# Eight feature tiles in the ring, the first query stack filled head by head, denominators turned before they are inverted

## The chip, the cores and the metric

One core of a Trainium2 chip. The metric is the device time of one execution in microseconds; the kernel before has 1396.77 us (median of 3 runs, 1396.46 to 1396.88).

## The reference

A layer on x of shape 8 x 1024 x 512 (8 batches, 1024 tokens, 512 features), all in float32: linear attention with random features, 16 heads of 32 columns and 128 features a head, then a ternary linear layer, with a layer norm after each.

```python
def feature_map(x, orf):                       # orf: 128 x 32
    proj = x @ orf.T / 32 ** 0.25
    norm = jnp.sum(x * x, axis=-1, keepdims=True) / (2.0 * math.sqrt(32))
    return (jnp.exp(proj - norm) + 1e-6) / math.sqrt(128)

q = feature_map(split(x @ Wq.T + bq), orf)     # split: 16 heads
k = feature_map(split(x @ Wk.T + bk), orf)
v = split(x @ Wv.T + bv)
kv, ksum = jnp.einsum('nlm,nld->nmd', k, v), jnp.sum(k, axis=1)
out = einsum('nlm,nmd->nld', q, kv) / einsum('nlm,nm->nl', q, ksum)
x = layernorm(x + out @ Wo.T + bo)
x = layernorm(x + x @ (ternary(W) * scale).T)
```

The division by the query features' product with ksum is the denominator of which the change speaks.

## The kernel before

Precision comes from splitting: a float32 operand is held as a high part rounded to fp32r and the rest as a low part, and three fp32r products (hi x hi, lo x hi, hi x lo) replace one float32 product. The features of a head are made from a stack in SBUF: rows of the projected unit's high and low parts and of its norms lie under one another, so that one or two matrix products give projection and norm together.

One list of stages, `SCHEDULE`, is walked by every engine's program in the same order, and each engine does its own part of a stage; so the list is the order of the instructions on every engine, and semaphores tie them. A batch is eight units: heads in four groups g, for each group a key unit (even u) and a query unit (odd u), and then the output stages. The lines that matter:

- `P` (L858): projection of a later unit, in four pieces of six products spread over a unit; `S` (ACT L582, L585) and `L` (DVE L756) take its high part, squares and low part out of PSUM. PSUM gives two banks to P, V, O and FF in turn.
- `LIFT` (SP, L427 to L451): copies the unit's high and low parts by DMA into the stack of its parity, 10 DMAs for a key unit and 12 for a query unit. `N` (PE L866, DVE L764 and L767) makes the norms and POOL's or SP's queue lifts them (L316, four DMAs). For unit 1 the wait is that of `NL`, and both wait for the last `FF` of the batch before (L434, L514), since the output stages use the same half of `ST` for the split attention (columns 0 to 2047) and the split rows (2048 to 3071); heads 0 to 3 of the stack lie at columns 0, 1024, 2048 and 3072.
- `F`: feature tile r of 0 to 7. PE makes the exponents (key: L821 with orf_key_a and orf_key_b, four products; query: L885, one), ACT takes the exponential (L601) into the ring `FE` of four tiles, and for a key unit DVE adds the tile to a running sum in `DR[:, 0]` (L718, L721). A key's tile r is one of token block r, a query's is head r % 4 of token half r // 4.
- `G` r (PE L898): 16 narrow float32 matmul records for two tiles, 128 x 32 weights, kv += features x values; the last, G 7, also multiplies the sum with ones (L904). In a key unit the pairs G 0,1, G 2,3 and G 4,5 stand between pieces of P and pairs of F; G 6,7 stand in the query unit after its F 0,1.
- `KVT` (PE L912, L913; DVE L771): kv and ksum turned; `GG` half (PE L927, 16 records): numerators into `ND[half]` and denominators into `DN`, four heads' 512 tokens each, every denominator repeated on its head's 32 partitions.
- After `GG`, ACT copies `DN` into `DR[:, h]` and adds the eps term (L621); stage `R` on DVE inverts 128 x 512 (L785) and multiplies (L787) into `VA`. In the last query unit and the output stages R comes in two halves of 256 columns.
- Output stages per token block: `A` split, `O` output product (L821 with Wo), `LN` (DVE L799 to L708, POOL L500, L502), `Y` and `ST` (ACT L549), `YT` transposes (PE L943, ACT L629, DVE L804), `FF` (L821 with W_ternary, DVE L809), and `V` (L844 to L846) of the next batch between them. In batch 0, unit 2 ends with `WF`, the ternary weights, on DVE (L693, L694).

## Time and profile before

| | us |
|---|---|
| median of 3 runs | 1396.77 |
| the profiled execution, its own time | 1395.43 |
| its span on the core (granted clock 0.991) | 1392.9 |
| PE busy, span share | 1335.7, 96% |
| DVE busy | 949.0, 68% |
| ACT busy | 741.5, 53% |
| POOL busy | 318.5, 23% |

The engines are PE (TensorE's products), PEld (its weight loads, beside PE), DVE (VectorE), ACT (ScalarE), POOL (GpSimd) and SP (SyncE, here a DMA queue). Products overlap: a product of 512 columns is shown 0.39 us long while the next starts 0.23 us after it, so that a stall is best read from the distance of two starts. A row of the timeline that merges instructions gives the start of the first and the end of the last. A batch takes 167.2 us in the middle of the run.

### The profile page before, as it was taken

Reading aid. Unit: us, or ns where it says so; the run is one execution under the profiler, and the core shown is the slowest. Engines: PE = TensorE matmul, PEld = TensorE weight load, DVE = VectorE, ACT = ScalarE, POOL = GpSimd, SP = SyncE. Lnnn points to the kernel's source line nnn. Section 1 sums busy time; section 2 is a strip of 40 time slices with the busy share of each in tenths; the row PEclk is TensorE's granted clock in tenths of the full one; section 3 lists DMA queues with packets and bytes.
Section 4 is the critical chain, followed back from the end, with each engine's and each line's share of the span. In section 5 each row is a group of like instructions: output and inputs, shape, how many; then the busy total and the mean of one; then the engine's idle time right before and its main releaser. Section 6 shows DMA issues by size and latency. Waiting matters only on the chain. (4 is left out here: it accounts for less than half of the span.)

```text
span 1392.9 us, 25111 instructions
## 1 busy us (share of the span) xinstructions
PE 1335.7 (96%) x9034; PEld 957.8 (69%) x9034; DVE 949.0 (68%) x1594; ACT 741.5 (53%) x1401; POOL 318.5 (23%) x573
## 2 busy tenths in 40 slices
PE   6999999999999999999999999999999999999885
PEld 5656677666776677666786667866677666776564
DVE  5468774787657776667756777567774687647684
ACT  5457535665355743557436663467535665355542
POOL 1011231113221222212322114211231112321232
PEclk9999999999999999999999999999999999999997
DMA  6566504673147720668116761267503673146511
GB/s 206 135 152 150 135 32 111 155 180 95 38 120 177 177 67 35 150 151 197 46 35 158 186 156 44 77 144 180 147 31 104 158 178 100 39 120 145 129 46 45
DMA packets 85562, 164.55 MB, mean 118 GB/s; under 512 B 20416, under 2 KB 37440, under 8 KB 84928
## 3 DMA queue, kind: packets, MB, share of 16 engines
q1 hardware_dynamic: 68480, 140.04, 39.5%
q10 hardware_dynamic: 9792, 17.12, 3.4%
q0 software_dynamic: 7168, 5.80, 3.2%
q8 instruction: 72, 1.18, 0.4%
q14 instruction: 50, 0.41, 0.1%
HBM read 39.13 MB, written 16.78 MB: 40 GB/s over the span
## 5 line engine op out<-in xcount | busy, mean ns | idle before, releaser
L601 ACT ACTIVATE features<-ps 128x512 f32<-128x512 f32 x512 | 278.1, 597 | 218.5 <-PE ps L821 166.9
L785 DVE RECIPROCAL den<-den 128x512 f32<-128x512 f32 (+1 forms) x80 | 216.6, 2708 | 44.6 <-ACT den L621 44.6
L316 POOL DMA_DIRECT2D stacks<-norm_rows x224 | 121.9, 550 | 542.9 <-DVE norm_rows L767 514.0
L721 DVE TENSOR_TENSOR den<-den,features 128x512 f32<-128x512 f32 x192 | 140.4, 731 | 93.5 <-ACT features L601 82.5
L500 POOL TENSOR_TENSOR stats<-stats,cols 128x1 f32<-128x1 f32 x128 | 79.3, 619 | 451.7 <-DVE stats L708 451.7
L821 PE MATMUL ps<-Wo_hi,stacks 128*128 128x512 f32 x512 | 173.4, 402 | 1.4 <-DVE rows L799 0.7
L574 ACT ACTIVATE values_then_attention<-ps 128x512 f32<-128x512 f32 x64 | 38.3, 599 | 196.6 <-PE ps L846 193.1
L821 PE MATMUL ps<-orf_key_a,stacks 128*128 128x256 f32 x512 | 140.8, 307 | 0.0
L821 PE MATMUL ps<-W_ternary,stacks 128*128 128x512 f32 x512 | 129.5, 396 | 7.2 <-DVE stacks L804 7.2
L927 PE MATMUL ps<-features,kv_ksum 128*32 128x512 f32 x1024 | 126.1, 610 | 5.2 <-DVE kv_ksum L771 3.4
L549 ACT ACTIVATE rows<-rows,stats 128x512 f32<-128x512 f32 x128 | 101.0, 813 | 54.8 <-POOL stats L502 54.6
L821 PE MATMUL ps<-orf_key_b,stacks 72*128 72x256 f32 x512 | 128.1, 281 | 0.0
L756 DVE SCALAR_TENSOR_TENSOR unit_lo<-ps,cols,unit_hi 128x512 fp32r<-128x512 f32 x128 | 95.5, 746 | 44.4 <-ACT squares L585 43.7
L821 PEld LDWEIGHTS ps<-Wo_hi,stacks 128*128 128x128 f32 x512 | 96.4, 188 | 34.4 <-issue 13.8
L821 PEld LDWEIGHTS ps<-orf_key_a,stacks 128*128 128x128 f32 x512 | 96.7, 189 | 29.4 <-issue 29.1
L821 PEld LDWEIGHTS ps<-W_ternary,stacks 128*128 128x128 f32 x512 | 96.8, 190 | 29.0 <-issue 5.1
L844 PE MATMUL ps<-Wv_hi,x_hi 128*128 128x512 f32 x256 | 103.2, 403 | 13.2 <-DVE x_lo L749 11.2
L858 PE MATMUL ps<-x_hi,Wq_hi 128*128 128x512 f32 x256 | 103.5, 404 | 0.2 <-DVE unit_lo L756 0.2
L582 ACT ACTIVATE unit_hi<-ps,cols 128x512 fp32r<-128x512 f32 x128 | 88.8, 694 | 24.9 <-PE ps L858 24.9
L858 PE MATMUL ps<-x_hi,Wk_hi 128*128 128x512 f32 x256 | 101.8, 398 | 0.0
L846 PE MATMUL ps<-Wv_hi,x_lo 128*128 128x512 f32 x256 | 100.5, 393 | 0.0
L845 PE MATMUL ps<-Wv_lo,x_hi 128*128 128x512 f32 x256 | 100.4, 392 | 0.0
(114 smaller groups left out, 2519.3 us busy)
## 6 DMA issues: line engine op xcount, KB each, us to landing
stacks<-unit_hi SPq DMA_DIRECT2D x384, 128.0 KB, 2.4
stacks<-unit_lo SPq DMA_DIRECT2D x256, 128.0 KB, 3.7
stacks<-unit_hi SPq DMA_DIRECT2D x64, 256.0 KB, 3.8
out<-rows ACTq DMA_DIRECT2D x64, 256.0 KB, 2.0
rows<-in_x_t SPq DMA_DIRECT2D x56, 256.0 KB, 3.9
rows<-in_x SPq DMA_DIRECT2D x32, 256.0 KB, 3.8
features<-in_x SPq DMA_DIRECT2D x32, 256.0 KB, 3.9
stacks<-norm_rows POOLq DMA_DIRECT2D x128, 32.0 KB, 3.3
```

Source lines behind the costliest of these rows:

```text
L316: queue.dma_start(dst[:, :, 256 * c:256 * (c + 1)], src.broadcast_to([NR, n, 256])).then_inc(sig.sem, 16)
L549: nc.scalar.activation(row, row, ACT.Identity, scale=ln(k, t, 10), bias=ln(k, t, 11))\
L601: nc.scalar.activation(FE[:, n % 4, :, 0:M], ps[:, :].rearrange("p (a m) -> p a m", a=HG), ACT.Exp, scale=C_EXP).then_inc(a_exp.sem, 1)
L721: ins = nc.vector.tensor_tensor(total, total, FE[:, r % 4, :, 0:M], ALU.add)
L756: nc.vector.scalar_tensor_tensor(out=EL[:, u % 2, half], in0=ps[:, :], scalar=BC[:, u:u + 1], in1=EH[:, u % 2, half].bitcast(F32), op0=ALU ...
L785: nc.vector.reciprocal(den, den).then_inc(v_rc.sem, len(parts))
L821: last = mm(out, a, b, start=(n == 0), stop=(n == len(terms) - 1))
L844: mm(ps[:, :], XH[:, k, c], WH["v"][:, k, :], start=(k == 0), stop=False)
L845: mm(ps[:, :], XH[:, k, c], WL["v"][:, k, :], start=False, stop=False)
L846: last = mm(ps[:, :], XL[:, k, c], WH["v"][:, k, :], start=False, stop=(k == KT - 1))
L858: last = mm(ps[:, :], *terms[n], start=(n == 0), stop=(n == len(terms) - 1))
L927: last = mm(bank[DH * h:DH * (h + 1), :], KVS[:, g % 2, c + DH * h:c + DH * (h + 1)], FE[:, h, :, 0:M], start=True, stop=True, tile_positi ...
```

## The change

- The ring `FE` has eight tiles in place of four, tile r of a unit always in slot r; the exponentials' waits follow. `dynamic_dma_scratch_size` is set to 4096 bytes.
- In a key unit G 0 to 3 stand together after F 4,5, and G 4 to 7 together in the query unit after F 0,1; the pieces of P move between the pairs of F, the last of them behind F 6,7.
- The stack of unit 1 is filled head by head, head 3 without a wait, heads 0 and 1 after the last `O`, head 2 after the last `FF`; `LIFT` of unit 1 moves ahead of the last `FF` in the list.
- ACT's copy of the denominators is gone. At `GG` DVE turns `DN` in blocks of 32 x 32 into `DR[:, h]`, adds the eps term to one column of each block (128 x 16), inverts these 16 columns, and at `R` turns them back, each read 32 times, before the product.

```diff
--- before.py
+++ after.py
@@ -87,9 +87,11 @@
     lift = [("LIFT", *two)] if two else []
     if is_key(u):
         st = [[("ST", b - 1, t)] if u == 0 and b else [] for t in (TT - 2, TT - 1)]
-        seq = f(0, 1) + (p[0] if u else []) + p[1] + s0 + l0 + [("G", b, g, 0), ("G", b, g, 1)] + f(2, 3) + st[0]
-        seq += p[2] + [("G", b, g, 2), ("G", b, g, 3)] + f(4, 5) + p[3] + s1 + [("G", b, g, 4), ("G", b, g, 5)]
-        seq += f(6, 7) + l1 + lift + st[1]
+        half = [("G", b, g, r) for r in range(4)]
+        if u == 0:
+            seq = f(0, 1) + p[1] + s0 + l0 + f(2, 3) + st[0] + p[2] + f(4, 5) + half + s1 + l1 + f(6, 7) + lift + st[1] + p[3]
+        else:
+            seq = f(0, 1) + p[0] + f(2, 3) + p[1] + s0 + l0 + f(4, 5) + half + p[2] + f(6, 7) + s1 + l1 + lift + p[3]
         if u == 0 and b == 0:
             seq += [("WA", 0, k) for k in range(KT)]
         if u == 2 and b == 0:
@@ -98,7 +100,7 @@
             seq += [("LX", b + 1, t) for t in range(4)]
         return seq
     norm = [("N", *later(1))] if later(1) else []
-    kv = [("G", b, g, 6), ("G", b, g, 7)] + norm
+    kv = [("G", b, g, r) for r in range(4, 8)] + norm
     if u < NU - 1:
         seq = p[0] + f(0, 1)
         if u == 1 and b == 0:
@@ -138,7 +140,7 @@
             seq += [("N", b + 1, 1)]
     seq += [("Y", b, TT - 1)] + v(TT - 1) + [("FF", b, TT - 2), ("ST", b, TT - 3), ("YT", b, TT - 1)]
     if more:
-        return seq + [("P", b + 1, 2, 0, 0), ("P", b + 1, 2, 0, 1), ("FF", b, TT - 1), ("LIFT", b + 1, 1), ("NL", b + 1)]
+        return seq + [("P", b + 1, 2, 0, 0), ("P", b + 1, 2, 0, 1), ("LIFT", b + 1, 1), ("FF", b, TT - 1), ("NL", b + 1)]
     return seq + [("FF", b, TT - 1), ("ST", b, TT - 2), ("ST", b, TT - 1)]
 
 
@@ -214,7 +216,7 @@
         ST = sb("stacks", [P, 2, 4 * L], F32R)
         EH, EL = sb("unit_hi", [P, 2, L], F32R), sb("unit_lo", [P, 2, L], F32R)
         SQ = sb("squares", [P, L])
-        FE = sb("features", [P, 4, HG, M + 1])
+        FE = sb("features", [P, 8, HG, M + 1])
         XR = sb("rows", [P, 4, D])
         BO = sb("out_bias", [P, D])
         ident = sb("ident", [P, P])
@@ -237,6 +239,8 @@
         SC, HS, NHS = col(25), col(26), col(27)
         RSUM, CC, WSUM = col(28, 2 * NG), col(36, 2 * NG), col(44, KT)
 
+        by_token = [col(64 + 16 * h, 16) for h in range(2)]
+
         stats = sb("stats", [P, 2, 4, 12])
 
         def ln(kind, t, a, n=1):
@@ -266,12 +270,13 @@
 
         a_xhi, a_v, a_p = Signal("x_hi_ready", TT), Signal("v_ready", TT), Signal("unit_hi_sq_ready", 4 * NU)
         a_exp, a_kc = Signal("features_ready", 8 * NU), Signal("kv_copied", 3 * NG)
-        a_den, a_ahi = Signal("den_copied", 2 * NG, 1), Signal("a_hi_ready", TT)
+        a_ahi = Signal("a_hi_ready", TT)
         a_y, a_yhi, a_out = Signal("y_ready", TT), Signal("y_hi_ready", TT), Signal("out_ready", TT)
 
         v_xlo, v_plo, v_n = Signal("x_lo_ready", TT), Signal("unit_lo_ready", 2 * NU), Signal("norms_ready", 2 * NU)
         v_ks = Signal("features_added", 7 * NG)
         v_kvc, v_c = Signal("kv_ready", NG), Signal("eps_sums_ready", NG)
+        v_dt, v_dr = Signal("den_turned", 2 * NG, 1), Signal("den_steps", 2 * 2 * NG)
         v_rc, v_a = Signal("reciprocal_ready", 2 * NG, 0, 2), Signal("attention_ready", 2 * NG, 2, 2)
         v_alo, v_ylo = Signal("a_lo_ready", TT, TT), Signal("y_lo_ready", TT, 2)
         v_ln = [Signal("ln1_steps", 5 * TT, 1), Signal("ln2_steps", 5 * TT, 4)]
@@ -324,7 +329,7 @@
         s_w = [sem(f"setup_w_{w}") for w in "kqof"]
 
 
-        staged_a = FE[:].rearrange("p a h m -> p (a h m)")[:, 0:KT * D].rearrange("p (k o) -> p k o", k=KT)
+        staged_a = FE[:, 0:4].rearrange("p a h m -> p (a h m)")[:, 0:KT * D].rearrange("p (k o) -> p k o", k=KT)
         raw = {"v": staged_a, "k": XR[:, :, :], "q": staged_a, "o": XR[:, :, :]}
         raw_ff = XR[:, :, :]
         orf_t = DR[:, 1, 0:P]
@@ -430,9 +435,19 @@
                     hi, lo, sig = EH[:, u % 2, :].bitcast(F32), EL[:, u % 2, :].bitcast(F32), lifted[u % 2]
 
                     wait(t_f.sem, t_f.nth(b, 8 * (u - 1)))
+                    wait(a_p.sem, a_p.nth(b, 4 * u + 3))
                     if u == 1:
-                        wait(t_ff.sem, t_ff.nth(b, 0))
-                    wait(a_p.sem, a_p.nth(b, 4 * u + 3))
+
+                        wait(v_plo.sem, v_plo.nth(b, 2 * u + 2))
+                        for h in (3, 0, 1, 2):
+                            if h == 0:
+                                wait(t_o.sem, t_o.nth(b, 0))
+                            elif h == 2:
+                                wait(t_ff.sem, t_ff.nth(b, 0))
+                            c = slice(L * h, L * (h + 1))
+                            for r, src in ((0, hi), (2 * DH, hi), (DH, lo)):
+                                sp.dma_start(slot[r:r + DH, c], src[DH * h:DH * (h + 1), :]).then_inc(sig.sem, 16)
+                        continue
                     for h in range(HG):
                         src = hi[DH * h:DH * (h + 1), :]
                         if is_key(u):
@@ -525,8 +540,6 @@
 
         @block.scalar
         def _(act):
-            for sig in (a_den,):
-                act.sem_inc(sig.sem, sig.credit)
             for sig in d_st:
                 act.sem_inc(sig.sem, sig.credit * sig.step)
 
@@ -590,15 +603,15 @@
 
                     if n == 0:
                         act.wait_ge(v_ln[0].sem, v_ln[0].nth(b, 0))
-                    v, r = (n - 4) // 8, (n - 4) % 8
-                    if n < 4:
+                    v, r = u - 1, at[1]
+                    if u == 0:
                         act.wait_ge(t_gg.sem, t_gg.nth(b, 0))
                     elif is_key(v):
                         act.wait_ge(t_g.sem, t_g.nth(b, 4 * v + r + 1))
                         act.wait_ge(v_ks.sem, v_ks.nth(b, 7 * (v // 2) + max(r, 1)))
                     else:
                         act.wait_ge(t_gg.sem, t_gg.nth(b, v - 1 + r // 4 + 1))
-                    nc.scalar.activation(FE[:, n % 4, :, 0:M], ps[:, :].rearrange("p (a m) -> p a m", a=HG),
+                    nc.scalar.activation(FE[:, n % 8, :, 0:M], ps[:, :].rearrange("p (a m) -> p a m", a=HG),
                                          ACT.Exp, scale=C_EXP).then_inc(a_exp.sem, 1)
                 elif kind == "G" and at[1] == 7:
                     kv = ND[0]
@@ -612,14 +625,6 @@
                                          accum_out=RSUM[:, 2 * u:2 * u + 1]).then_inc(a_kc.sem, 1)
                     nc.scalar.activation(KVT[:, M:2 * M], kv[:, 2 * M:3 * M], ACT.Identity, bias=EPSL,
                                          accum_out=RSUM[:, 2 * u + 1:2 * u + 2]).then_inc(a_kc.sem, 1)
-                elif kind == "GG":
-                    g, h = u, at[1]
-                    act.wait_ge(t_gg.sem, t_gg.nth(b, 2 * g + h + 1))
-                    if h == 0:
-                        act.wait_ge(v_c.sem, v_c.nth(b, g + 1))
-                    act.wait_ge(v_a.sem, v_a.nth(b, 2 * g + h - 1))
-                    nc.scalar.activation(DR[:, h, :], DN[:, :], ACT.Identity,
-                                         bias=CC[:, 2 * g + 1:2 * g + 2]).then_inc(a_den.sem, 1)
                 elif kind == "A":
                     split_hi(b, u)
                 elif kind == "Y":
@@ -636,7 +641,7 @@
 
         @block.vector
         def _(dve):
-            for sig in (v_a, v_alo, v_ylo, v_ln[0], v_ln[1]):
+            for sig in (v_a, v_alo, v_ylo, v_ln[0], v_ln[1], v_dt):
                 dve.sem_inc(sig.sem, sig.credit * sig.step)
             chain = [0]
 
@@ -718,7 +723,7 @@
                     ins = nc.vector.tensor_tensor(total, FE[:, 0, :, 0:M], FE[:, 1, :, 0:M], ALU.add)
                 else:
                     dve.wait_ge(v_ks.sem, v_ks.nth(b, 7 * g + r - 1))
-                    ins = nc.vector.tensor_tensor(total, total, FE[:, r % 4, :, 0:M], ALU.add)
+                    ins = nc.vector.tensor_tensor(total, total, FE[:, r, :, 0:M], ALU.add)
                 ins.then_inc(v_ks.sem, 1)
 
             def split_lo(b, t):
@@ -775,14 +780,28 @@
                     dve.wait_ge(a_kc.sem, a_kc.nth(b, 3 * u + 3))
                     nc.vector.tensor_scalar(CC[:, 2 * u:2 * u + 2], RSUM[:, 2 * u:2 * u + 2], EPS, None,
                                             ALU.mult).then_inc(v_c.sem, 1)
+                elif kind == "GG":
+                    g, h = u, at[1]
+                    n, turned, den = 2 * (2 * g + h), DR[:, h, :], by_token[h]
+                    dve.wait_ge(t_gg.sem, t_gg.nth(b, 2 * g + h + 1))
+                    dve.wait_ge(v_a.sem, v_a.nth(b, 2 * g + h - 1))
+                    nc.vector.transpose(turned, DN[:, :]).then_inc(v_dt.sem, 1)
+                    dve.wait_ge(v_dt.sem, v_dt.nth(b, 2 * g + h + 1))
+                    dve.wait_ge(v_c.sem, v_c.nth(b, g + 1))
+                    nc.vector.tensor_scalar(den, turned.rearrange("p (a c) -> p a c", c=DH)[:, :, 0], CC[:, 2 * g + 1:2 * g + 2],
+                                            None, ALU.add).then_inc(v_dr.sem, 1)
+                    dve.wait_ge(v_dr.sem, v_dr.nth(b, n + 1))
+                    nc.vector.reciprocal(den, den).then_inc(v_dr.sem, 1)
                 elif kind == "R":
                     g, h = u, at[1]
-                    dve.wait_ge(a_den.sem, a_den.nth(b, 2 * g + h + 1))
+                    dve.wait_ge(v_dr.sem, v_dr.nth(b, 2 * (2 * g + h) + 2))
 
                     parts = [at[2]] if len(at) > 2 else [0, 1]
                     t0, t1 = 2 * parts[0], 2 * parts[-1] + 2
                     den = DR[:, h, P * t0:P * t1]
-                    nc.vector.reciprocal(den, den).then_inc(v_rc.sem, len(parts))
+                    n = HG * (t1 - t0)
+                    of_tokens = by_token[h][:, HG * t0:HG * t1].unsqueeze(2).broadcast_to([P, n, DH])
+                    nc.vector.transpose(den.rearrange("p (a c) -> p a c", c=DH), of_tokens).then_inc(v_rc.sem, len(parts))
                     dve.wait_ge(v_rc.sem, v_rc.nth(b, 2 * g + h) + parts[-1] + 1)
                     nc.vector.scalar_tensor_tensor(
                         out=VA[:, 4 * h + t0:4 * h + t1, P * g:P * (g + 1)],
@@ -895,7 +914,7 @@
                         pe.wait_ge(v_a.sem, v_a.nth(b, max(2 * u - 1, 0)))
                     for h in range(HG):
                         rows = slice(DH * h, DH * (h + 1))
-                        last = mm(kv[rows, 0:M + 1], VA[:, r, P * u + DH * h:P * u + DH * (h + 1)], FE[:, r % 4, h, :],
+                        last = mm(kv[rows, 0:M + 1], VA[:, r, P * u + DH * h:P * u + DH * (h + 1)], FE[:, r, h, :],
                                   start=(r == 0), stop=(r == 7), tile_position=(0, DH * h), skip_group_check=True)
                     if r == 7:
                         pe.wait_ge(v_ks.sem, v_ks.nth(b, 7 * u + 7))
@@ -906,7 +925,7 @@
                     last.then_inc(t_g.sem, 1)
                 elif kind == "KVT":
                     pe.wait_ge(a_kc.sem, a_kc.nth(b, 3 * u + 3))
-                    pe.wait_ge(a_den.sem, a_den.nth(b, 2 * u))
+                    pe.wait_ge(v_dt.sem, v_dt.nth(b, 2 * u))
                     if b == 0 and u == 0:
                         pe.wait_ge(s_bo, 1)
                     nc.tensor.transpose(DN[:, 0:P], KVT[:, 0:M], ident[:, :])
@@ -920,12 +939,12 @@
                         pe.wait_ge(v_a.sem, v_a.nth(b, 2 * g))
                         if b == 0 and g == 0:
                             pe.wait_ge(s_scale, 1)
-                    pe.wait_ge(a_den.sem, a_den.nth(b, 2 * g + half))
+                    pe.wait_ge(v_dt.sem, v_dt.nth(b, 2 * g + half))
                     pe.wait_ge(a_exp.sem, a_exp.nth(b, 16 * g + 8 + 4 * half + 4))
                     for bank, c in ((DN, P), (ND[half], 0)):
                         for h in range(HG):
                             last = mm(bank[DH * h:DH * (h + 1), :], KVS[:, g % 2, c + DH * h:c + DH * (h + 1)],
-                                      FE[:, h, :, 0:M], start=True, stop=True, tile_position=(0, DH * h))
+                                      FE[:, HG * half + h, :, 0:M], start=True, stop=True, tile_position=(0, DH * h))
                     last.then_inc(t_gg.sem, 1)
                 elif kind == "O":
                     pe.wait_ge(v_alo.sem, v_alo.nth(b, u + 1))
@@ -976,7 +995,7 @@
                 "Wo_t": weight("attn_Wo"), "ffn_t": weight("ffn_weight"), "bias_columns": bias, "bo": given("attn_bo"),
                 "orf_t": _np.tile(given("attn_orf").T, (4, 1))}
 
-    nc = _bacc.Bacc("TRN2", target_bir_lowering=False, num_devices=1)
+    nc = _bacc.Bacc("TRN2", target_bir_lowering=False, num_devices=1, dynamic_dma_scratch_size=4096)
     arrays, args = {}, []
     for name, a in laid_out.items():
         a = _np.ascontiguousarray(a)
```

## Rows read from the trace of the kernel before

**Rows 1.** Page, part 1: busy us, share of the span, instructions.

```profile
PE 1335.7 (96%) x9034; PEld 957.8 (69%) x9034; DVE 949.0 (68%) x1594; ACT 741.5 (53%) x1401; POOL 318.5 (23%) x573
```

**Rows 2.** Windows: length; busy (count) PE, PEld, DVE, ACT, POOL; PEclk; DMA; GB/s.

```profile
224.00:391.00 167.00, 164.88 (x1128) 118.86 (x1128) 115.52 (x193) 90.80 (x172) 38.57 (x68) 1.00 0.47 119
...
100.00:101.90 1.90, 1.80 (x12) 0.53 (x16) 0.70 (x2) 0.00 (x0) 1.53 (x3) 0.55 0.88 298
```

**Rows 3.** Waits of PE, whole span: waiter, releaser, total us, times, longest.

```profile
PE ps L885 <- issue: 4.7, 6, 1.2
...
PE ps L927 <- DVE kv_ksum L771: 3.4, 2, 2.7
PE ps L904 <- DVE den L721: 2.8, 7, 0.5
PE ps L844 <- DVE rows L799: 2.0, 7, 0.3
```

**Rows 4.** Timeline of PE, key unit (b=1, u=2): start, duration, instruction, merged count.

```profile
254.87 0.39 PE L858 MATMUL ps<-x_hi,Wk_lo 128*128 128x512 f32 x1
255.09 0.39 PE L858 MATMUL ps<-x_lo,Wk_hi 128*128 128x512 f32 x1
255.41 0.65 PE L898 MATMUL ps<-features,values_then_attention 128*32 128x129 f32 x16
255.99 0.39 PE L821 MATMUL ps<-orf_key_a,stacks 128*128 128x256 f32 x1
256.22 0.28 PE L821 MATMUL ps<-orf_key_b,stacks 72*128 72x256 f32 x1
256.33 0.28 PE L821 MATMUL ps<-orf_key_a,stacks 128*128 128x256 f32 x1
```

**Rows 5.** Timeline of PE, start of the first query unit (b=1, u=1).

```profile
239.06 0.70 PE L885 MATMUL ps<-stacks,orf_query 104*128 104x512 f32 x2 [0.54 <-issue]
239.69 0.65 PE L898 MATMUL ps<-features,values_then_attention 128*32 128x129 f32 x16
240.16 0.40 PE L904 MATMUL ps<-den,ones 128*32 128x128 f32 x8
```

**Rows 6.** Timeline of SP's queue: the stack of unit (b=1, u=1).

```profile
226.87 0.61 SPq L442 DMA_DIRECT2D stacks<-unit_hi  x1
...
232.86 3.94 SPq L451 DMA_DIRECT2D stacks<-unit_lo  x4
```

**Rows 7.** Timeline of POOL: norm rows of units (1, 1) and (1, 2).

```profile
230.59 2.21 POOL L316 DMA_DIRECT2D stacks<-norm_rows  x4 [0.50 <-issue]
...
243.41 2.18 POOL L316 DMA_DIRECT2D stacks<-norm_rows  x4 [10.61 <-DVE norm_rows L767]
```

**Rows 8.** Page, part 6: a DMA issue's count, KB, median us from issue to landing.

```profile
stacks<-norm_rows POOLq DMA_DIRECT2D x128, 32.0 KB, 3.3
```

**Rows 9.** Timeline of PE: first product of key unit (b=1, u=2).

```profile
251.53 0.39 PE L821 MATMUL ps<-orf_key_a,stacks 128*128 128x256 f32 x1
```

**Rows 10.** Groups by line: busy us, mean ns, idle before and its releaser.

```profile
L601 ACT ACTIVATE features<-ps 128x512 f32<-128x512 f32 x512 | 278.1, 597 | 218.5 <-PE ps L821 166.9 <-PE ps L885 50.4 <-DVE den L721 1.2
L785 DVE RECIPROCAL den<-den 128x512 f32<-128x512 f32 (+1 forms) x80 | 216.6, 2708 | 44.6 <-ACT den L621 44.6
...
L621 ACT ACTIVATE den<-ps,cols 128x512 f32<-128x512 f32 x64 | 44.1, 690 | 74.2 <-PE ps L927 73.4
L804 DVE TENSOR_TENSOR stacks<-ps,stacks 128x512 fp32r<-128x512 f32 x64 | 44.0, 687 | 53.7 <-ACT stacks L629 53.7
...
L707 DVE TENSOR_SCALAR stats<-stats 128x1 f32<-128x1 f32 x128 | 19.7, 154 | 4.8 <-DVE stats L705 0.4
```

**Rows 11.** Line 785 alone: min/median/max ns, start of first and last.

```profile
L785 DVE RECIPROCAL den<-den x80: 1741/3344/3355, 74.5 to 1349.5; 128x512 f32<-128x512 f32 x48, 128x256 f32<-128x256 f32 x32
```

**Rows 12.** Timeline of PE: first GG of the second head group, batch 0.

```profile
100.10 3.61 PE L927 MATMUL ps<-features,kv_ksum 128*32 128x512 f32 x16 [2.73 <-DVE kv_ksum L771]
```

**Rows 13.** Chain of work that ended last: start, us, what (batch 7's tail).

```profile
1322.77 1.76 DVE den L785
```

## Prediction

> **What bounds the kernel.** I read the page's busy times first: PE 96% of the span, DVE 68%, ACT 53% [rows 1]. Then the windows, since a share is a mean: in one whole batch PE is busy 164.9 of 167.0 us at full clock [rows 2]. So the kernel is as long as PE's stream of products, and an edit is worth what it takes out of that stream or out of PE's few stalls; a faster DVE or ACT is worth nothing of itself. The waits of PE name the stalls [rows 3]. What no view of waits shows is time lost between products when PE changes from one kind to another; for that I read starts in PE's timeline [rows 4].
>
> All sums are made against the profiled execution (1395.43 us, span 1392.9); the median of the runs is 1.3 us above it, and the result is given on the median.
>
> **1. G in fours.** In the timeline of a key unit products of P start 0.22 to 0.23 us apart, but the first of G 0,1 comes 0.32 us after the last P: 0.09 lost on entry. G 0,1 then hold PE 0.58 us (255.41 to 255.99) [rows 4], while the pair G 6,7, which is followed by more products of its own kind, takes 0.47 (239.69 to 240.16) [rows 5]: 0.11 lost on leaving. And the first product of F after G blocks the next for 0.23 us (255.99 to 256.22), where the following one takes 0.11 (256.22 to 256.33) [rows 4]: 0.11 more. So each visit to G costs 0.31 by rows rounded to 0.01, and I take 0.29, since 0.47 for a pair contains one change less than a pair that stands alone and rounding goes both ways. The key unit had three visits and has one; the query unit keeps its one, which is longer but not more frequent. The new visit goes from F to G and from G to P, an order that before hardly shows; I price it like the old one, with 0.2 to 0.4 as bounds. That is 2 x 0.29 = 0.58 us for a key unit. It counts in 31 of 32; in the last one, batch 7 without P beside it, PE waits for ACT and for the lift of the last unit anyway. **31 x 0.58 = 18.0 us**, 14 to 20 with the bounds.
>
> Does the new order wait anywhere? G 0 to 3 need the exponentials 0 to 3; F 2,3 lie a whole piece of P (1.37 us, six starts of 0.23) ahead, and two exponentials take 1.2 [rows 10]. F 6 needs the bank of exponential 4, and G (about 1.0) and P lie between. The sum on DVE has the moved P and two more tiles of G ahead of G 7, some 1.9 us more than before. Eight slots let key tile 4 be written before G 0 has run, so nothing ties F to G any longer. I cost the order itself at nothing. If that cover failed the exponential would be late by at most its own 0.6 us per pair.
>
> **2. The first query stack.** SP may begin only when the last FF is done: first copy at 226.87, the last four start between 232.86 and 236.8 [rows 6], and PE's first F of the unit sits idle 0.54 us until 239.06 [rows 5]. Over the run this is the line 4.7 us, 6 times, put down to issue [rows 3] (a DMA's landing). An idle PE also loses the overlap: products 0.39 us long follow at 0.23 [rows 4], so 0.16 more each time: 4.7 + 6 x 0.16 = **5.7 us**. After the change nine of the twelve copies are out before the last FF, three remain (1.8 us of issue instead of 9.9). What is next is POOL's norm rows, which still wait for the last FF: issued 230.59 to 232.8, landing 3.3 after issue [rows 7, 8], so about 236; F of unit 1 is due at 239.06 - 0.54 - 0.16 - 0.58 = 237.8. It fits with some 1.5 us, so the gain is kept whole; a landing as slow as 5.3 would leave 0.3 a batch.
>
> **3. Denominators.** Off ACT: 64 copies of 690 ns. Off DVE: 80 reciprocals, 216.6 us [rows 10], 1.74 us for 256 columns and 3.35 for 512 [rows 11], hence 6.3 ns a column and 0.14 fixed. On DVE instead, per half: a turn of 128 x 512 out of PSUM, no such operation in the trace; nearest is a tensor-tensor of 128 x 512 from PSUM, 687 ns, and the bounds are that and the old reciprocal's 3.35; I take 0.69. Then an add of 16 columns (154 ns for one [rows 10], 0.17), a reciprocal of 16 (0.14 + 16 x 6.3 ns = 0.24), and the turn back, 0.69 (0.42 for a half). A half is 1.8 instead of 3.35 on DVE and 0.69 on ACT: DVE loses about 100 us of 949, ACT 44. PE does not wait for these but through the cases below.
>
> The vector rule that bears on this speaks against it: the Trainium skill, VectorE: DVE Perf Modes, Rules for kernel authors, says to keep the number of chained DVE operations small since each ends in a pipeline flush, and here one operation becomes four. By that rule the stage would grow; by the reciprocal's row it shrinks, and the row decides. For the turn itself the Trainium skill, Vector Engine (DVE) Microarchitecture Reference, section 3.8, gives one element a cycle and lane, the rate of a plain copy; by it the sum is the one above.
>
> Where it reaches PE: **G 7** waits for DVE's running sum, 2.8 us in 7 [rows 3], with the overlap 2.8 + 7 x 0.16 = **3.9 us**, gone by part 1's slack and the shorter R ahead of the sums. **V of token block 3** waits 7 times for DVE's rows of LN, which stand behind a half reciprocal: 2.0 + 7 x 0.16 = **3.1 us**, gone with it (1.74 becomes 0.42). **Batch 0, second GG** waits 2.73 us behind the ternary weights on DVE and then takes 3.61 us where 1.9 is usual [rows 12], at a granted clock of 0.55 [rows 2] after PE had stood idle: 4.6 us in all. DVE comes to that work about 1.4 us earlier against PE; I take **2.5 us** (1.4, and part of the clock), bounds 1 and 4.6. **The tail**: a half reciprocal of 1.76 lies on the chain that ended last [rows 13], ACT's copy of 0.69 before it, and two more of 1.67 follow in the chain: 0.69 + 1.76 becomes about 1.6, and the two become 0.42 each, 3.4 us, less 0.5 because G 4,5 now stand behind the last lift, and less what PE itself bounds: **2.4 us**, bounds 0 and 5.
>
> One wait is added: DVE stands at GG until PE has finished it. Behind it are R, and N of unit u + 2, about 1.1 us later than before; its norm rows have a whole unit's time. PE's KVT and GG now wait for DVE's first turn in place of ACT's copy, which comes at the same point. SP's waits are the same but for the head-by-head ones; nothing is queued behind head 3 before the last O. The smaller DMA scratch I cost at nothing, see the second rival. LIFT's new place in the list moves nothing: SP has no part in FF.
>
> **Sum.** 18.0 + 5.7 + 3.9 + 3.1 + 2.5 + 2.4 = 35.6 us. 1395.4 - 35.6 = 1359.8, on the median 1361.
>
> **Rivals.** *Only part of the visits' price comes back.* The loss might be tied to what follows G: P after G could lose more than F did, or F to G cost more than P to G, or exponentials come late in the packed order. At half, 9 us less: **1370**. For it: the new pair of neighbours is nearly unseen. Against: entry and exit were each read by themselves, and other changes of kind show like sizes. Chance 0.12.
>
> *The norm rows land late, slower than before.* POOL builds its descriptors in the scratch that shrinks to 4096 bytes. If issue and landing of four copies, now 2.2 + 3.3 - 0.5 = 5 us [rows 7, 8], doubled, key units would wait: for unit 2 of batch 1, issued from 243.41 [rows 7], rows land near 248.4 and F begins at 251.53 [rows 9], 3.1 us of slack. Of 5 us more, 1.9 would remain, on 24 units (2, 4, 6 of eight batches) and, with the 1.5 us of part 2, 3.5 on 8: 46 + 28 = 74 us, so 1361 + 74 = **1435**. It decides from 3.1 us of delay per lift on, and makes the kernel slower than before from 3.8 (24 x 0.7 + 8 x 2.3 = 35). Against: each of these copies is only 32 KB in few rows, and they come four in ten us. Chance 0.04.
>
> *The turn is slow*, as slow as the reciprocal (3.35 each way). DVE would gain 7 us a half over today, about 400 us, and DVE would be the bound in query units: around **1440**. Against: it is a move of data. Between 0.7 and 1.5 us the turn changes nothing but parts of 3.9, 3.1, 2.5 and 2.4, giving 1365. Chance of the slow end 0.02, of the middle 0.07.
>
> *More than counted.* The visits at 0.31, batch 0's stall gone whole, the tail at 5, and small waits behind DVE and ACT which the freer engines shorten: 36 + 1.2 + 2.1 + 2.6 + 1 to 3 = 43 to 45, **1353**. Chance 0.15.
>
> **Numbers.** Forecast as summed 0.60, at 1361 (1356 to 1366). The range takes in the first rival and the last and ends at 1352 and 1373. A measurement can tell about 0.2% from no change: faster 0.93, same 0.01, slower 0.06 (both slow rivals, none of which has to reach its price).
>
> **What would show it.** In PE's timeline of a key unit: one merged row of 32 records of L898, some 1.3 us long, and no other; a batch period of 167.2 - 4 x 0.58 - 0.7 to 0.8 - 0.6 - 0.45 = about 163.2 us. In PE's waits: no issue wait at L885, no L904 behind DVE, no L844 behind L799. In the lines: turns near 0.69, a reciprocal near 0.24, DVE busy near 850, ACT near 697. Wrong would be: an idle mark before G 0 or F 6 in the packed order, an issue wait at L821's key features (late norm rows), or a turn over 1 us.

## The result and the profile after

| | before | after |
|---|---|---|
| median | 1396.62 us (4 runs) | 1351.61 us (4 runs, 1348.68 to 1353.47) |
| profiled execution, its own time | 1395.43 | 1348.68 |
| its span | 1392.9 | 1346.9 |

The ratio is 0.967, 95% interval 0.9654 to 0.9691: 3.3% faster. The forecast was 1361 (1352 to 1373), 35.6 us of gain; the median is 0.4 us under the range, the gain 45 us by the medians and 46.0 by the two spans. The direction and most of the terms were right; the sum was about 10 us short.

The page's first part, as in [rows 1]. PE has lost 26 us of busy time; DVE 95 and ACT 43, as forecast (about 100 and 44).

```profile
PE 1310.0 (97%) x9034; PEld 972.9 (72%) x9034; DVE 853.5 (63%) x1786; ACT 698.3 (52%) x1337; POOL 312.9 (23%) x573
```

PE's waits after the change, the whole span (waiter, releaser, total us, times, longest), against [rows 3]. Line numbers have moved: L840, L904, L917, L946 are lines 821, 885, 898 and 927 of before. The issue wait of the query features (line 885 of before) is gone; so are the wait of G 7 (line 904 of before) for the running sum and that of V for LN's rows. The wait of 3.2 us is one, the lift of the very last unit; the one behind kv_ksum has shrunk from 3.4 to 1.6.

```profile
PE ps L863 <- DVE x_lo L754: 11.1, 1, 11.1
PE ps L840 <- DVE stacks L823: 7.3, 4, 2.5
PE ps L904 <- DMA stacks<-unit_lo: 3.2, 1, 3.2
PE ps L946 <- ACT features L614: 1.8, 2, 1.0
PE ps L946 <- DVE kv_ksum L776: 1.6, 2, 1.1
```

PE's timeline in the key unit of [rows 4]: its first product, its visit to G, and the first product of the next key unit. One visit of 32 records, 247.48 to 248.50, 1.02 us for four tiles (0.58 for two before). In: 0.21 from the last orf_key_b product, where the next would come after 0.12. Out: P's first product keeps the next waiting 0.34 instead of 0.23. Four tiles in 1.02 is also 0.08 more than twice the 0.47 that a pair takes when more of its kind follow [rows 5].

```profile
241.62 0.39 PE L840 MATMUL ps<-orf_key_a,stacks 128*128 128x256 f32 x1
...
247.27 0.28 PE L840 MATMUL ps<-orf_key_b,stacks 72*128 72x256 f32 x1
247.48 1.09 PE L917 MATMUL ps<-features,values_then_attention 128*32 128x129 f32 x32
248.50 0.50 PE L877 MATMUL ps<-x_hi,Wk_hi 128*128 128x512 f32 x1
248.84 0.40 PE L877 MATMUL ps<-x_hi,Wk_lo 128*128 128x512 f32 x1
...
266.58 0.39 PE L840 MATMUL ps<-orf_key_a,stacks 128*128 128x256 f32 x1
```

From 241.62 to 266.58 two units take 24.96 us. Before, the same pair ran from 251.53 [rows 9] to 277.05, 25.52 us:

```profile
277.05 0.39 PE L821 MATMUL ps<-orf_key_a,stacks 128*128 128x256 f32 x1
```

So this pair of units is 0.56 us shorter, against 0.58 forecast. By the same starts, with the known waits taken off, it is 0.6 in the pair of units 6 and 7 and 0.7 in that of units 0 and 1. A batch, from the first key product of one to that of the next, takes 162.67 us (218.04 to 380.71), where 163.2 was forecast.

The denominators: first the two turns' own lines (min/median/max ns, starts), then the groups of the two small operations (busy us, mean ns, idle before); the old row is in [rows 10, 11]. A turn is 0.71 us from PSUM as from SBUF, where 0.69 was taken; the 16-column operations are 0.24 and 0.25 (0.17 and 0.24 taken).

```profile
L804 DVE STREAM_TRANSPOSE den<-cols x80: 435/705/714, 72.9 to 1309.0; 128x512 f32<-128x512 f32 x48, 128x256 f32<-128x256 f32 x32
...
L788 DVE STREAM_TRANSPOSE den<-ps x64: 705/717/720, 71.5 to 1289.1; 128x512 f32<-128x512 f32 x64
```

```profile
L794 DVE RECIPROCAL cols<-cols 128x16 f32<-128x16 f32 x64 | 16.2, 254 | 2.2
L791 DVE TENSOR_SCALAR cols<-den,cols 128x16 f32<-128x16 f32 x64 | 15.2, 237 | 2.3
```

What no forecast term had, first: the end of the program. These rows are of line 201 (203 after), the block's closing instructions, min/median/max ns and start. Before, POOL's drain starts with its last work at 1384.2 and ends at 1392.7, while ACT, whose last store is the last thing of use, is through at 1387.6. In both kernels that is 3.4 us after POOL's drain begins, so only what the drain takes beyond 3.4 us lengthens the span: 5.1 us before, 0.5 after. First the kernel before, then after.

```profile
L201 POOLq DRAIN  x1: 8492/8492/8492, 1384.2 to 1384.2; - x1
...
L201 ACTq DRAIN  x1: 8/8/8, 1387.6 to 1387.6; - x1
```

```profile
L203 POOLq DRAIN  x1: 3917/3917/3917, 1342.7 to 1342.7; - x1
...
L203 ACTq DRAIN  x1: 8/8/8, 1346.1 to 1346.1; - x1
```

Second, a wait in batch 0. Behind F 0,1 of unit 1 PE multiplies sums of the ternary weights that ACT makes (L837; the stage is put behind the end of unit 0 for ACT). In PE's waits of the kernel before it has this row:

```profile
PE ps L837 <- ACT W_ternary L564: 1.3, 1, 1.3
```

After the change there is none: the last piece of P now stands between F 6,7 of unit 0 and this product, and ACT has that time.

### The profile page after: what moved, and what is told of

It reads as the page before. It is cut to its first block, busy times and chain, and to the rows that moved or that the text cites. A ratio compares the mean times of both kernels' runs of the same rounds, so it can differ in the third digit from the quotient of the medians.

```text
span 1346.9 us, 25311 instructions
## 1 busy us (share of the span) xinstructions
PE 1310.0 (97%) x9034; PEld 972.9 (72%) x9034; DVE 853.5 (63%) x1786; ACT 698.3 (52%) x1337; POOL 312.9 (23%) x573
## 4 chain that ended last, share of the span: by engine, by line
PE 91%; ACT 3%; DVE 3%; issue 1%; DMA 1%; SPq 1%; ACTq 0%; POOL 0%; DVEq 0%; POOLq 0%
PE ps L840 30%; PE ps L877 26%; PE ps L946 9%; PE ps L863 4%; PE ps L865 4%; PE ps L864 4%; PE ps L917 4%; PE ps L904 4%; PE ps L962 2%; PE ps L885 1%; ACT kv_ksum_t L626 1%; PE ps L931 1%; ACT kv_ksum_t L624 1%; DMA values_then_attention<-in_x_t 1%; DVE stats L707 1%
## 5 line engine op out<-in xcount | busy, mean ns | idle before, releaser
L840 PE MATMUL ps<-Wo_hi,stacks 128*128 128x512 f32 x512 | 173.5, 402 | 0.6 <-DVE stacks L731 0.2
L726 DVE TENSOR_TENSOR den<-den,features 128x512 f32<-128x512 f32 x192 | 132.8, 691 | 56.3 <-ACT features L614 42.6
L840 PE MATMUL ps<-W_ternary,stacks 128*128 128x512 f32 x512 | 128.8, 394 | 7.3 <-DVE stacks L823 7.3
L840 PE MATMUL ps<-orf_key_a,stacks 128*128 128x256 f32 x512 | 131.9, 289 | 0.4 <-ACT features L614 0.4
L840 PE MATMUL ps<-orf_key_b,stacks 72*128 72x256 f32 x512 | 128.4, 282 | 0.0
L946 PE MATMUL ps<-features,kv_ksum 128*32 128x512 f32 x1024 | 123.1, 598 | 3.5 <-ACT features L614 1.8
L840 PEld LDWEIGHTS ps<-Wo_hi,stacks 128*128 128x128 f32 x512 | 96.1, 188 | 33.2 <-issue 13.4
L840 PEld LDWEIGHTS ps<-W_ternary,stacks 128*128 128x128 f32 x512 | 96.7, 190 | 28.9 <-issue 4.9
L840 PEld LDWEIGHTS ps<-orf_key_a,stacks 128*128 128x128 f32 x512 | 97.1, 190 | 16.4 <-issue 11.5
L877 PE MATMUL ps<-x_hi,Wk_hi 128*128 128x512 f32 x256 | 104.5, 408 | 0.0
L877 PE MATMUL ps<-x_lo,Wq_hi 128*128 128x512 f32 x256 | 101.1, 395 | 0.0
L877 PE MATMUL ps<-x_lo,Wk_hi 128*128 128x512 f32 x256 | 100.6, 393 | 0.0
L877 PE MATMUL ps<-x_hi,Wk_lo 128*128 128x512 f32 x256 | 100.6, 393 | 0.0
```

The costliest lines, as they stand in the source:

```text
L726: ins = nc.vector.tensor_tensor(total, total, FE[:, r, :, 0:M], ALU.add)
L840: last = mm(out, a, b, start=(n == 0), stop=(n == len(terms) - 1))
L877: last = mm(ps[:, :], *terms[n], start=(n == 0), stop=(n == len(terms) - 1))
L946: last = mm(bank[DH * h:DH * (h + 1), :], KVS[:, g % 2, c + DH * h:c + DH * (h + 1)], FE[:, HG * half + h, :, 0:M], start=True, stop=True, ...
```

## Experiments

Each ratio is to the kernel before, on the same chip, with its 95% interval. A difference to the changed kernel is one of medians from different rounds; the kernel before had 1396.6 to 1398.3 in them, so such a difference is good to about 2 us.

**The DMA scratch alone.** In the kernel before:

```diff
-    nc = _bacc.Bacc("TRN2", target_bir_lowering=False, num_devices=1)
+    nc = _bacc.Bacc("TRN2", target_bir_lowering=False, num_devices=1, dynamic_dma_scratch_size=4096)
```

> The kernel before with the DMA scratch cut from its default of 16384 bytes to 4096, nothing else. In both traces POOL's last instruction, a drain after all work, ends the span: 8.49 us long before, 3.92 after the change. Theory A, its length goes with the size of the scratch: drain near 3.9 us, time 4.6 us under the kernel before (ratio 0.9967). Rival B, the drain waits for something else that the change made shorter (norm rows, the last unit): drain stays at 8.5 us, time unchanged. Rival C, less room slows POOL's DMAs: issue to landing of the norm rows above 3.3 us, time above the kernel before.

Measured 1392.01 us, ratio 0.9952 (0.9934 to 0.9971), and the drain of the changed kernel again:

```profile
L201 POOLq DRAIN  x1: 3917/3917/3917, 1386.2 to 1386.2; - x1
```

The norm rows land after a median of 3.4 us (3.3 before). So theory A's cause holds and B and C fall: the smaller scratch alone makes the drain 4.6 us shorter, and the kernel 4 to 9 us faster by the interval.

**8192 and 1024 bytes** in the changed kernel.

> The changed kernel with a scratch of 8192 bytes instead of 4096. Theory A, on the line through 8.49 us at 16384 and 3.92 at 4096 (0.372 us per 1024 bytes, 2.43 at none): drain 5.4 us, time 1.5 us above the changed kernel. Rival B: drain stays 3.9, time the same.

> The changed kernel with a scratch of 1024 bytes. Theory A: drain 2.8 us, time 1.1 us under the changed kernel. Rival C, here the room is a sixteenth of the default: POOL's four norm copies take longer than 2.2 us of issue and 3.3 to landing, key units wait, time up. Rival B: same time.

With 8192: 1357.04 us, 0.9699 (0.9667 to 0.9732), drain 8.8 us. With 1024: 1350.66 us, 0.9652 (0.9617 to 0.9687), drain 0.98 us. ACT's last store now sets the end, 3.4 us after the drain begins, so the shorter drain can be worth 0.5 us at most; the span is 2.1 us under the changed kernel's, but POOL's last work already ends 1.5 us earlier there (1341.2 for 1342.7), which is a difference between executions. POOL's issue (0.55 us each) and landing (3.3) are unchanged even at 1024. First 8192, then 1024:

```profile
L203 POOLq DRAIN  x1: 8815/8815/8815, 1345.1 to 1345.1; - x1
```

```profile
L203 POOLq DRAIN  x1: 977/977/977, 1341.2 to 1341.2; - x1
```

The straight line of my expectation is refuted: 5.4 was expected at 8192, and it is longer than at 16384; 2.8 was expected at 1024. Two more runs of the kernel before, for a rule, one execution each: a scratch of 2048, and one of 16384 with POOL issuing fewer DMAs:

```diff
-                elif kind == "N" and at[0] == 0:
-                    lift_norms(sp, wait, n_first, b, 0)
+                elif kind == "N" and is_key(at[0]):
+                    lift_norms(sp, wait, n_lifted[0] if at[0] else n_first, b, at[0])
...
-                if kind == "N" and t > 1:
+                if kind == "N" and t % 2 and t > 1:
```

> The kernel before with a scratch of 2048 bytes. Drain 0.98 us at 1024 and 3.92 at 4096, in proportion: 1.96 us expected. If it has steps instead, 0.98 or 3.92.

> The kernel before (scratch 16384) with the norm rows of the key units 2, 4, 6 issued by SP: POOL issues 128 DMAs instead of 224, about 0.7 of the descriptors. If the closing drain goes over what POOL has written into its scratch up to its size: 6 us or less instead of 8.49. If it is a fixed cost above some size: 8.5 us.

At 2048 the drain is 0.65 us, under that of 1024; the one execution took 1396.08 us, which shows no gain, and one execution can't (those of the kernel before spread from 1394.7 to 1403.3). With 128 DMAs instead of 224 the drain is 10.8 us, longer, and the kernel is at 1422 us: PE waits 7.5 us for ACT's squares and 3.4 for norm rows, neither of which it did before. That SP's queue, now with waits for the norms in it, holds these up is argued, not shown. Both expectations missed:

```profile
L201 POOLq DRAIN  x1: 650/650/650, 1390.5 to 1390.5; - x1
```

```profile
L201 POOLq DRAIN  x1: 10777/10777/10777, 1408.3 to 1408.3; - x1
```

The length repeats within 3 ns in kernels with the same scratch and the same POOL DMAs (8.49 three times, 3.92 in all six with 4096, 0.98 twice), so it hangs on these two; by what rule is open.

**The visits.** The changed kernel with the key unit's old order:

```diff
-            seq = f(0, 1) + p[0] + f(2, 3) + p[1] + s0 + l0 + f(4, 5) + half + p[2] + f(6, 7) + s1 + l1 + lift + p[3]
+        seq = f(0, 1) + (p[0] if u else []) + p[1] + s0 + l0 + [("G", b, g, 0), ("G", b, g, 1)] + f(2, 3) + st[0]
+        seq += p[2] + [("G", b, g, 2), ("G", b, g, 3)] + f(4, 5) + p[3] + s1 + [("G", b, g, 4), ("G", b, g, 5)]
+        seq += f(6, 7) + l1 + lift + st[1]
...
-    kv = [("G", b, g, r) for r in range(4, 8)] + norm
+    kv = [("G", b, g, 6), ("G", b, g, 7)] + norm
```

> The changed kernel with the old order of the key unit (G 0,1, G 2,3, G 4,5 between P and F, G 6,7 in the query unit), ring of eight, new stack filling, new denominators and small scratch kept. By the price of a visit, 0.29 us, twice in 31 key units: 18 us slower than the changed kernel, about 1370. If, as the starts of the units suggest (1.01 less in a key unit, 0.39 to 0.46 more in a query unit), the visits gave 0.62: 19.2 us. Rival, the visits were worth half and the freed DVE and ACT gave the rest: 9 us. The stalls at KVT in unit 5 and at G 7 in unit 7, which went away, should come back in part only if they hung on the order; by freed engines they stay away.

Measured 1381.81 us, 0.9881 (0.9842 to 0.992): 30 us above the changed kernel, far more than the 18 to 19 expected. PE's waits say why:

```profile
PE ps L929 <- ACT kv_ksum_t L624: 5.8, 15, 0.5
PE ps L921 <- DVE den L724: 3.5, 7, 0.8
PE ps L944 <- DVE kv_ksum L774: 2.7, 1, 2.7
PE ps L854 <- ACT W_ternary L575: 1.3, 1, 1.3
```

The stalls of KVT, of G 7, of batch 0's GG and of the ternary weights are all back, with DVE and ACT as free as in the changed kernel. So the order removed them, not the new denominators. What they cost against the changed kernel I read from the starts of the same products in the two traces, since a wait mark for KVT overstates it (the changed kernel has a hidden one there, see the last experiment): KVT 3.9 us (0.44 in unit 5 of seven batches, 0.1 in unit 1 of eight), G 7 4.6, GG 3.2, the ternary weights 1.4. The visits make the rest, 20.8 us: 0.67 for a key unit in 31. The tail gives 1 us back. Together this is the 33 us between the two spans. Per key unit the visits cost 0.67 here and 0.56 to 0.7 between the kernel before and the changed one; why the middle units differ is open.

**The old denominators** in the changed kernel (ACT's copy, 128 x 512 reciprocal).

```diff
-                    nc.vector.transpose(den.rearrange("p (a c) -> p a c", c=DH), of_tokens).then_inc(v_rc.sem, len(parts))
+                    nc.vector.reciprocal(den, den).then_inc(v_rc.sem, len(parts))
...
+                elif kind == "GG":
+                    ...
+                    nc.scalar.activation(DR[:, h, :], DN[:, :], ACT.Identity,
+                                         bias=CC[:, 2 * g + 1:2 * g + 2]).then_inc(a_den.sem, 1)
```

> The changed kernel with the old denominators: ACT copies them, DVE inverts 128 x 512. The forecast's terms that hang on the denominators are V of token block 3 (3.1 us, 7 times), the tail (2.4) and part of batch 0 (1 to 2): 6 to 7 us slower than the changed kernel. G 7's 3.9 us stay gone if the order did it. Rival, the denominators give nothing to a kernel bound by PE: under 2 us. Other rival, they carry also the stall at KVT in unit 5 (3.1 us): 9 to 10 us.

Measured 1363.74 us, 0.9757 (0.9728 to 0.9785): 12 us above the changed kernel, twice the expectation.

```profile
PE ps L873 <- DVE unit_lo L771: 3.2, 8, 0.4
PE ps L919 <- DVE den L736: 2.0, 6, 0.5
PE ps L859 <- DVE rows L814: 1.8, 7, 0.3
```

V's wait is back as forecast (1.8 + 7 x 0.16 = 2.9). Two waits are there besides: in the new order P waits for DVE's low part at the end of unit 6 (3.2 + 8 x 0.16 = 4.5), and G 7 for the sum (2.0 + 6 x 0.16 = 3.0), since DVE is late again. The first had cost the kernel before 0.2 us, once: the new order needs the lighter DVE.

**The old filling of the first query stack** in the changed kernel, and **the new filling alone** in the kernel before.

```diff
-                    wait(a_p.sem, a_p.nth(b, 4 * u + 3))
                     if u == 1:
-                        wait(v_plo.sem, v_plo.nth(b, 2 * u + 2))
-                        for h in (3, 0, 1, 2):
-                            ...
+                        wait(t_ff.sem, t_ff.nth(b, 0))
+                    wait(a_p.sem, a_p.nth(b, 4 * u + 3))
```

> The changed kernel with the first query stack filled as before, all twelve copies behind the last FF. Theory: F of unit 1 is due 0.6 us earlier than in the kernel before and the stack lands where it did, so its wait comes back larger: 7 times the old wait and 0.6 more, or 5.7 + 4.2 = about 10 us slower than the changed kernel. If the new filling was worth only what was forecast in the kernel before: 5.7 us. Rival, the norm rows bound it anyway: under 2 us.

> The kernel before with the new filling of the first query stack alone. Forecast by its stalls: 5.7 us faster, ratio 0.9959, and no issue wait at the query features' product. Rival, norm rows are late next (due about 12 us after F of unit 0, landing 9 to 11 after it): 3 us or less.

The first: 1367.46 us, 0.9786 (0.9757 to 0.9815), 16 us above the changed kernel where about 10 was expected. PE waits for the stack 15.6 us in 8; one of them, 3.2, is the last unit's, which the changed kernel has too. The other seven are 1.1 to 3.5 us long:

```profile
PE ps L894 <- DMA stacks<-unit_lo: 8.3, 4, 3.2
...
PE ps L894 <- issue: 7.3, 4, 3.5
```

The second: 1390.37 us, 0.9954 (0.9939 to 0.997), 6.2 us faster than before (5.7 forecast), and among PE's waits none for issue at the query features. The norm rows were not next in line. The wait that goes is not the same in every execution: with the filling and the order of before it adds up to 4.0 us in the run with the small scratch, 4.7 in the trace of the forecast, 5.8 at 2048 bytes.

**ACT's kv copies ahead of the next batch's x block**, in the kernel before. The row that my forecast had left out is this one of PE's waits, the copies before KVT:

```profile
PE ps L912 <- ACT kv_ksum_t L613: 4.5, 9, 0.5
```

```diff
-            seq += xt(0) + kv + f(2, 3) + [("KVT", b, g)] + p[1] + s0 + l0 + xt(1, 2, 3)
+            seq += kv + xt(0) + f(2, 3) + [("KVT", b, g)] + p[1] + s0 + l0 + xt(1, 2, 3)
```

> The kernel before with one stage moved: in the unit 5 of each batch ACT's and DVE's split of the next batch's first x block comes behind the group's G and N instead of ahead. Theory: KVT's extra wait of 0.44 us in that unit (7 times, 3.1 us) is ACT doing that split (0.65 us) before the kv copies; it goes, 3.1 us faster. Rival: the wait is the copies' own chain, which G 7 starts: nothing changes.

Measured 1397.0 us, 1.0001 (0.9982 to 1.002): no change. The wait itself did what theory said:

```profile
PE ps L912 <- ACT kv_ksum_t L613: 0.8, 2, 0.5
...
PE ps L904 <- DVE den L721: 5.0, 7, 1.2
PE ps L927 <- DVE kv_ksum L771: 4.5, 9, 2.7
```

Seven of nine waits at KVT are gone: in unit 5 KVT starts 0.44 us earlier against the F pair before it. GG has seven new waits (9 for 2), and these are the edit's own doing. It moved DVE's part of the split as well, so that DVE's copy of the turned kv, which GG needs, now stands behind it; in the kernel before this copy starts 0.91 us after KVT (293.21 to 294.12), here 1.52 (294.91 to 296.43):

```profile
295.82 0.68 DVE L749 TENSOR_TENSOR x_lo<-rows,x_hi 128x512 fp32r<-128x512 f32 x1
296.43 0.42 DVE L771 COPY kv_ksum<-ps 128x256 f32<-128x256 f32 x1
```

The longer wait of G 7 (5.0 for 2.8) can't be put down to the edit: the runs with a smaller scratch and the old order have 4.2 and 4.8 there. That ACT's split delayed KVT is shown; what this stall is worth alone is not, since the edit moved DVE's part with ACT's.

**One visit for all eight G**, which the ring of eight allows. First behind the first piece of P in the query unit:

```diff
-        seq = p[0] + f(0, 1)
+        seq = p[0] + kv + f(0, 1)
```

with `kv` all of G 0 to 7 and N.

> The changed kernel with all eight G of a group in one visit, at the start of the query unit behind the first piece of P; the eight slots allow it. By the price of a visit (0.29 us) 31 visits less: 9 us faster than the changed kernel; and KVT now has F 0 to 3 between itself and G 7, so its wait for ACT's copies (some 0.15 us, 31 times) goes: together 12 to 14 us, about 1338. Rival, packing so much float32 work makes the running sum or the exponentials late: PE idle before G 7 or F 2 of the query unit, gain under 5 us or a loss.

Measured 1366.44 us, 0.9777 (0.975 to 0.9804), 15 us slower than the changed kernel:

```profile
PE ps L903 <- ACT features L613: 18.6, 33, 0.6
```

The rival held, by another wait than I named first: F 0 to 3 of the query unit now stand back to back on two banks, and ACT has its kv copies and then the exponentials to do. Then with the piece of P between the pairs of F:

```diff
-        seq = p[0] + f(0, 1)
+        seq = kv + f(0, 1) + p[0]
...
-    nc = _bacc.Bacc("TRN2", target_bir_lowering=False, num_devices=1, dynamic_dma_scratch_size=4096)
+    nc = _bacc.Bacc("TRN2", target_bir_lowering=False, num_devices=1, dynamic_dma_scratch_size=1024)
```

> All eight G and N in one visit at the start of the query unit, now with a piece of P between F 0,1 and F 2,3, and a scratch of 1024 bytes. The one-visit kernel before this lost because F 0 to 3 stood back to back and PE waited 33 times for ACT's exponential (18.6 us shown). Theory: with 1.37 us of P between the pairs that wait goes; one visit less at 0.3 us in 31 units is 9 us, the shorter drain 2 to 3: about 1339 to 1341. Rival: G 7 now comes only one piece of P after F 7 and waits for DVE's sum, or the query stack lands too late: PE idle there, result not under 1349.

Measured **1332.99 us**, 0.9537 (0.9522 to 0.9553), 19 us under the changed kernel by the medians (15.9 by the spans of the two profiled executions) and the fastest of all, with 1.4 us of waits left at the query features. The smaller scratch in it is worth 0.5 us at most, by the run with 1024 bytes:

```profile
PE ps L903 <- ACT features L613: 0.7, 2, 0.5
PE ps L903 <- issue: 0.7, 1, 0.7
```

It gave more than the 10 to 12 us expected. Two key units start 0.65 us closer than in the changed kernel, in three of a batch's four head groups (0.1 or less in the first). A visit is 0.3 of it; the rest is KVT. In PE's timeline of the same unit (b=1, u=1), changed kernel first, then this one, KVT comes 0.83 us after the start of the pair of F ahead of it (230.98 to 231.81), and now 0.47 (228.02 to 228.49), since ACT's copies have a piece of P more to be done in:

```profile
230.98 0.72 PE L904 MATMUL ps<-stacks,orf_query 104*128 104x512 f32 x2
231.81 0.33 PE L931 MATMUL ps<-ident,kv_ksum_t 128*128 128x128 f32 x1
```

```profile
228.02 0.63 PE L903 MATMUL ps<-stacks,orf_query 104*128 104x512 f32 x2
228.49 0.27 PE L930 MATMUL ps<-ident,kv_ksum_t 128*128 128x128 f32 x1
```

So in every query unit the changed kernel waits some 0.36 us for ACT's copies, where PE's idle mark shows nothing; in the trace of before KVT comes 0.8 us after its F pair too, but in unit 5, where it is 1.26.

## Why the prediction came out as it did

Stage by stage from the starts of the same products in the two traces, beside the forecast:

| term | forecast | measured |
|---|---|---|
| visits to G, 31 key units | 18.0 | 18.7 (0.56 to 0.7 each) |
| first query stack | 5.7 | 5.7 |
| G 7 of unit 7 | 3.9 | 4.0 |
| V of token block 3 | 3.1 | 3.4 |
| batch 0, second GG | 2.5 | 3.3 |
| tail from the last query unit | 2.4 | 2.2 |
| KVT of unit 5 | none | 3.1 |
| ternary weights, batch 0 | none | 1.4 |
| POOL's closing drain | none | 4.6 |
| sum | 35.6 | 46.4, for 46.0 between the spans |

The measured terms add up to 0.4 too much; 0.2 to 0.3 of it is one stage that got longer, the second GG of unit 5 in batch 0.

**The visits** were right, in kind and size, though F to G and G to P had hardly been seen: entry 0.09, leaving and first product some 0.2 by the rows above. The way there was sound: a cost that stands in no view of waits, read from starts, times the count. **The stack** was right, run by itself too. What the sum could not say is that its price depends on the order around it: with F of unit 1 due earlier the old filling costs 16 us, not 5.7, and the 0.6 us by which F is due earlier explain 4 us of the difference, not all.

**The step that failed first** is the sentence "the smaller DMA scratch I cost at nothing, see the second rival". I weighed only whether it could hurt, and gave the hurt 0.04; the bound on the other side was left out. It gave 4.6 us, nearly half of the miss. The trace of before showed it: the last ACT instruction ended at 1387.6 and the span at 1392.9, and I never asked what filled the 5.3 us. The second rival is refuted down to 1024 bytes.

**The second** is the list of PE's stalls in parts 2 and 3. It took four of the rows of PE's waits and left out two that the change reached. One is KVT's, 4.5 us in 9: the new order gives ACT two tiles of G more before the copies are due, 0.44 us, seven times, 3.1 us. The other is that for the ternary weights in batch 0, 1.3 us idle and 0.16 of overlap. The run with the old order shows both back. Drain, KVT and the ternary weights make 9.1 us, which is the miss but for about 1 us spread over the other terms.

**G 7** was right in size, and of the two causes given, the order and the shorter R, the runs show the order to be enough with the new denominators; with the old ones 2.0 us of waits are back in six units, so it needs both. **Batch 0** was mis-sized, 2.5 for 3.3: GG runs at a granted clock of 1.00 there (0.55 before [rows 2]), taking 1.9 us after an idle of 1.12 where it took 3.61 after 2.73 [rows 12]:

```profile
95.68 1.91 PE L946 MATMUL ps<-features,kv_ksum 128*32 128x512 f32 x14 [1.12 <-DVE kv_ksum L776]
```

**The turn** was taken at 0.69 and is 0.71. Four operations of 0.71, 0.24, 0.25 and 0.71 replace one of 3.35, and DVE's total fell as said, so the rule of the Trainium skill to keep chained operations few (VectorE: DVE Perf Modes, Rules for kernel authors), which the prediction names, did not decide here. The rival of a slow turn did not come, and its price was wrong: two turns of 3.35 and two small operations of 0.4 are 7.1 us a half, which is 3.8 more than the old reciprocal and not 7, so 240 us and not 400. **The last rival**, more than counted, at 1353, was the nearest to what came, with the wrong items in it. The range failed at its lower end since that end was made of the counted terms and small waits only.

## What to carry to other kernels

Where one engine bounds a kernel, count how often it changes between kinds of work: here each visit to the narrow float32 products cost 0.3 us that no list of waits showed, and a longer ring was what allowed fewer visits. A list of stalls is to be taken whole, and each is worth only what the next engine in line lets through; removal runs overlap, so 33 + 16 + 21 us of span for taking back three parts one by one stand against 46 for all. Look at what ends the span after the last useful instruction, too.

## What the runs showed of the hardware

- POOL's closing drain changes with the scratch set aside for its DMAs, but not steadily: 8.5 us at 16384 bytes (default), 8.8 at 8192, 3.9 at 4096, 0.65 at 2048, 0.98 at 1024, and 10.8 at 16384 with 128 DMAs instead of 224. POOL's DMAs themselves, 224 of up to 32 KB, were as fast at 1024 bytes (0.55 us of issue, 3.3 to landing).
- PE goes from fp32r products of full width to float32 products of 32 columns and back for about 0.3 us (0.28 to 0.35 by the pairs of units above). Further tiles in the same visit cost 0.22 to 0.24 each.
- A turn of 128 x 512 float32 in blocks of 32 x 32 on DVE takes 0.71 us, out of PSUM or out of 16 columns of SBUF each read 32 times; a reciprocal costs 6.3 ns a column (1.74 us for 256, 3.35 for 512).
